# Graph attention: mask added on TensorE, plain maxima on VectorE, shorter per-engine steps; buffer rings of six and 122 edge groups instead of rings of four and 124

## The reference, cut to what matters

```python
# attention by angle, 4 layers
logits = beta * jnp.sum(h_norm[src] * h_norm[dst], axis=-1)
m = segment_max(logits, dst);  ex = exp(logits - m[dst])
out = segment_sum(ex / (segment_sum(ex, dst)[dst] + EPS) * h[src], dst)

# graph attention, 3 layers, 4 heads of 64
h = (x @ W).reshape(n, HEADS, C)
e = leaky_relu(s_src[src] + s_dst[dst], 0.2)      # s_src = <h, a_s>, s_dst = <h, a_d>
m = segment_max(e, dst);  ex = exp(e - m[dst])
out = segment_sum(h[src] * (ex / segment_sum(ex, dst)[dst]), dst) + b
```

## Time and profile before

| | us |
|---|---|
| three timed runs | 9922.85, 9924.49 (median), 9927.99 |
| profiled execution, its own time | 9927.93 |
| span, first to last instruction, of the profiled execution | 9926.2 |
| one layer of attention by angle, start to start (3896.8 to 6148.6 is three) | 750.6 |
| one layer of graph attention, start to start (6966.4 to 8902.0 is two) | 967.8 |
| PE busy over the span | 7005.6 (71%) |
| DVE busy over the span | 5926.7 (60%) |
| POOL busy over the span | 5383.8 (54%) |

### The profile page before, as it was taken

One profiled execution on the slowest core, in us unless ns is written; L12 is line 12 of the kernel. 1 busy time (PEld: TensorE's weight loads), 2 busy tenths in 40 slices (PEclk: granted clock), 3 DMA queues, 4 the chain that ended last, 5 costly groups with the idle time before them and its releaser, 6 DMA issues. The chain is left out here.

```text
span 9926.2 us, 160244 instructions
## 1 busy us (share of the span) xinstructions
PE 7005.6 (71%) x34788; PEld 5407.3 (54%) x34789; DVE 5926.7 (60%) x21625; ACT 2633.9 (27%) x6946; POOL 5383.8 (54%) x5578
## 2 busy tenths in 40 slices
PE   0003545535663982996996996996799989998997
PEld 0003445534442872885885885885466556655664
DVE  6003334442213225887887887887687768777777
ACT  0001100000000221222222222222455555555554
POOL 0675777747731112775775775774355445534553
PEclk9997557767775996998998998998677677776776
DMA  1301114453440991445445445444333323333333
GB/s 76 137 2 43 48 42 101 101 68 105 105 52 23 345 315 52 100 99 83 100 98 83 100 99 83 100 99 62 74 78 77 66 76 78 78 59 84 77 77 64
DMA packets 621385, 896.33 MB, mean 90 GB/s; under 512 B 289911, under 2 KB 427383, under 8 KB 620062
## 3 DMA queue, kind: packets, MB, share of 16 engines
q0 software_dynamic: 244928, 618.96, 28.9%
q1 hardware_dynamic: 376414, 276.94, 9.2%
HBM read 767.30 MB, written 135.40 MB: 91 GB/s over the span
## 5 line engine op out<-in xcount | busy, mean ns | idle before, releaser
L1510 POOL DMA_INDIRECT hs<-tab_agnn,rec x1984 | 1964.8, 990 | 1114.8 <-issue 593.9
L1944 POOL DMA_INDIRECT hs<-tab_gat,rec x1488 | 1406.4, 945 | 1282.6 <-DVE msg L2013 868.1
L2120 PE MATMUL psV<-msg,ohf 128*128 128x260 f32 x2976 | 1270.9, 603 | 0.8 <-DVE msg L2013 0.8
L1982 DVE CUSTOM_DVE_ANT_0 cand<-psL,neg 128x512 f32<-128x512 f32 x1488 | 991.5, 685 | 265.4 <-issue 176.4
L1531 DVE CUSTOM_DVE_ANT_0 prod<-psG,hs 128x256 f32<-128x256 f32 x1984 | 842.3, 480 | 421.1 <-DMA hs<-tab_agnn,rec 342.8
L2120 PEld LDWEIGHTS psV<-msg,ohf 128*128 128x128 f32 x2976 | 901.0, 317 | 204.1 <-issue 1.2
L1660 PE MATMUL psV<-hs,pr 128*128 128x258 f32 x3968 | 986.1, 392 | 6.2 <-DVE pr L1570 6.2
L1636 PE MATMUL psG<-HN,ohT 128*128 x3968 | 955.6, 384 | 5.1 <-ACT neg L1605 5.1
L626 PE MATMUL psT<-ident,oh 128*128 128x128 f32 x496 | 126.7, 405 | 1023.6 <-DVE oh L592 1023.6
L1636 PEld LDWEIGHTS psG<-HN,ohT 128*128 128x128 f32 x3968 | 725.6, 193 | 86.7 <-issue 6.1
L1660 PEld LDWEIGHTS psV<-hs,pr 128*128 128x128 f32 x3968 | 715.8, 190 | 89.5 <-DVE acc L1557 7.8
(11 more groups left out here) (326 smaller groups left out, 13438.2 us busy)
## 6 DMA issues: line engine op xcount, KB each, us to landing
w<-in_L_gnn_w SPq DMA_DIRECT2D x224, 512.0 KB, 6.0
fwd_d<-acc SPq DMA_DIRECT2D x10, 3224.0 KB, 44.2
fw<-fwd_d SPq DMA_DIRECT2D x124, 260.0 KB
hs<-tab_agnn,rec POOLq DMA_INDIRECT x1984
hs<-tab_gat,rec POOLq DMA_INDIRECT x1488
rec<-rec_d SPq DMA_DIRECT2D x1240, 8.0 KB, 1.7
b<-in_L_gnn_b SPq DMA_DIRECT2D x113, 128.0 KB, 6.4
x<-xbuf SPq DMA_DIRECT2D x112, 128.0 KB, 6.0
```

What stands on the lines that cost most here:

```text
L1510: nc.gpsimd.indirect_dma_start(out=hs[:, j, g, :], out_offset=None, in_=k.tab_agnn, in_offset=bass.IndirectOffsetOnAxis(ap=rec[:, j, g, 0: ...
L1944: nc.gpsimd.indirect_dma_start(out=hs[:, j, g, :], out_offset=None, in_=k.tab_gat, in_offset=bass.IndirectOffsetOnAxis(ap=rec[:, j, g, 0:1 ...
L1982: V.tensor_tensor_reduce(cand[:, m, :], psL[:, m, :], neg[:, h2, :], 1.0, -BIG, ALU.add, ALU.max, mt[:, h2, m:m + 1]).then_inc(s_lt, 1)
L2120: mm = nc.tensor.matmul(psV[:, h4, 0:W_GAT], ohf[:, h4, g, :], msg[:, h4, g, :], start=(g == 0), stop=(g == G - 1))
```

## The change

- **122 groups and rings of six.** `NG` is no longer rounded up to a multiple of the ring, `U` is 6, and `pipeline` appends the rest of the steps after the loop. The experts keep a ring of four (`UE`).
- **A row of zeros for pads.** Every gathered table gets one row more, number NP, which is zero, and pads name it. `sort_edges` sends unused records out of bounds, with a bounds check on the scatter. Logits of pads need no clamp any more: `below` goes from both attentions.
- **The mask is added on PE.** For each head a matmul of the identity with `neg` (now bf16, 512 columns, 128 rows) opens the accumulation in `psL`, and the 12-row matmul follows in it. DVE takes a plain maximum of two heads at a time.
- **No float copy of the one-hot.** PE transposes `away` in place of `oh`; ACT makes `oh` in fp32 four steps later, directly for `psV`.
- **Fewer, joined DVE operations.** Edge logits and node state share one tile `raw` and one slope operation; the block's sums are scaled in one operation and added in another; `msg` is made in one piece; ACT instead of DVE copies the peak.
- **Lags.** DVE works with lags 3, 4 and 6, PE with 1, 2, 3 and 5, ACT with 0, 1, 3 and 4.

```diff
-U = 4
+U = 6
 NG = (E + NB * (GE - 1)) // GE
-NG += -NG % U
...
+                nc.vector.memset(padrec[:, :, 0:1], NP).then_inc(s_pad, 1)
...
-                                in_=slot[:, n, g, 0:4], in_offset=None).then_inc(s_sent[n], 16)
+                                in_=slot[:, n, g, 0:4], in_offset=None, bounds_check=SPARE - 1,
+                                oob_is_err=False).then_inc(s_sent[n], 16)
...
-                                    V.tensor_tensor_reduce(cand[:, m, :], psL[:, m, :], neg[:, h2, :], 1.0, -BIG, ALU.add, ALU.max,
-                                                           mt[:, h2, m:m + 1]).then_inc(s_lt, 1)
+                                    V.tensor_reduce(mt[:, h2, m:m + 2], psL[:, m:m + 2, :], AX.X, ALU.max).then_inc(s_lt, 1)
...
+                            if add:
+                                dve.wait_ge(q.rs, flow(t6) + 1)
...
+                                V.tensor_tensor(a4, a4, b3(rs[:, j6, :], CH1), ALU.mult).then_inc(s_am, 1)
...
+                            if old:
+                                dve.wait_ge(s_leak, step_of(t + 1) + 1)
+                                V.tensor_tensor(g3(t3, h), g3(leaky, now), q3[:, :, 1, :], ALU.subtract).then_inc(q.tt, 1)
...
+                            if add:
+                                dve.wait_ge(q.v, nth(t6) + 1)
+                                dve.wait_ge(s_am, own(t6) + 1)
+                                V.tensor_tensor(acc, acc, psV[:, j6 % 2, 0:W_GAT], ALU.add).then_inc(q.u, 1)
...
-                                    nc.tensor.matmul(psL[:, m, :], sel[0:PARTS, m, :], sT[:, h1, :], start=True, stop=True).then_inc(q.b, 1)
+                                    nc.tensor.matmul(psL[:, m, :], k.identb[:, :], neg[:, h2, :], start=True, stop=False)
+                                    mm = nc.tensor.matmul(psL[:, m, :], sel[0:PARTS, m, :], sT[:, h2, :], start=False, stop=True)
```

More of the change, by code:

```diff
@@ L119, in lagged, with pipeline @@
     return i2, j2, t
-def pipeline(eng, step, drain, total=NG, numbers=None):
+def pipeline(eng, step, drain, total=NG, numbers=None, ring=U):
+    whole = total // ring
     if numbers:
         numbers.load(0)
-    for j in range(U):
+    for j in range(ring):
         step(0, j)
-    with eng.Fori(1, total // U) as i:
+    with eng.Fori(1, whole) as i:
         if numbers:
             numbers.load(i)
-        for j in range(U):
+        for j in range(ring):
             step(i, j)
-    if numbers and drain:
-        numbers.load(total // U)
-    for j in range(drain):
-        step(total // U, j)
+    for n in range(total % ring + drain):
+        if numbers and n % ring == 0:
+            numbers.load(whole + n // ring)
+        step(whole + n // ring, n % ring)
     if numbers:
@@ L1167, in experts @@
         s_ys = sem("s_ys")
-        s_out = [sem(f"s_out{n}") for n in range(U)]
+        s_out = [sem(f"s_out{n}") for n in range(UE)]
         s_gate = sem("s_gate")
@@ L1221, in step @@
                     pool.dma_start(k.ybuf_t[ds(t, 1), :, :].rearrange("a p c -> (a p) c"), y[:, n, :]).then_inc(s_out[n], 16)
-                pipeline(pool, step, 0, MT)
-                for n in range(U):
-                    pool.wait_ge(s_out[n], MT // U * 16)
+                pipeline(pool, step, 0, MT, ring=UE)
+                for n in range(UE):
+                    pool.wait_ge(s_out[n], MT // UE * 16)
             @block.vector
@@ L1265, in step @@
                         g.then_inc(s_g, 1)
-                pipeline(act, step, 1, MT)
+                pipeline(act, step, 1, MT, ring=UE)
             @block.tensor
@@ L1303, in step @@
                         mm.then_inc(s_y, 1)
-                pipeline(pe, step, 2, MT)
+                pipeline(pe, step, 2, MT, ring=UE)
 def combine(nc, k, a):
@@ new lines, in step @@
+                            top(1)
+                            if add:
+                                dve.wait_ge(q.rs, flow(t6) + 1)
+                                if not (isinstance(t6, int) and t6 < 1):
+                                    dve.wait_ge(q.u, nth(t6))
+                                a4 = acc.rearrange("p (h c) -> p h c", h=HEADS)
+                                V.tensor_tensor(a4, a4, b3(rs[:, j6, :], CH1), ALU.mult).then_inc(s_am, 1)
+                            if mid_:
+                                dve.wait_ge(s_lt, pairs(t2) + 2)
+                                V.tensor_tensor(at_block(smax, b), at_block(smax, b), mt[:, h2, :], ALU.max).then_inc(s_mx, 1)
+                                dve.wait_ge(s_mx, own(t2) * 2 + 1)
+                                V.tensor_tensor(raw[:, now, GH:], at_block(smax, b), at_block(sd, b), ALU.add).then_inc(s_mx, 1)
@@ new lines, in step @@
+                            if mid_ or old:
+                                if old:
+                                    dve.wait_ge(s_lg, own(t) + 1)
+                                if mid_:
+                                    dve.wait_ge(s_mx, own(t2) * 2 + 2)
+                                    if not (isinstance(t2, int) and t2 < 1):
+                                        dve.wait_ge(q.m, flow(t2))
+                                part = slice(0 if old else GH, GH + HEADS if mid_ else GH)
+                                V.scalar_tensor_tensor(out=leaky[:, now, part], in0=raw[:, now, part], scalar=NEG_SLOPE,
+                                                       in1=raw[:, now, part], op0=ALU.mult, op1=ALU.max).then_inc(s_leak, 1)
@@ new lines, in step @@
+                            if now:
+                                i0, _, t0 = now
+                                act.wait_ge(q.rec[j], use(i0, j) * 16 + 16)
+                                if not (isinstance(t0, int) and t0 < U):
+                                    act.wait_ge(q.t, flow(t0 - U + 1))
+                                    act.wait_ge(q.oh, nth(t0 - U + 1))
+                                for g in range(G):
+                                    ins = nc.scalar.activation(away[:, j, g, :], k.iota[:, :], ACT.Abs, bias=recf[:, j, g, 1:2], scale=-1.0)
+                                ins.then_inc(s_away, 1)
@@ L2090, in _ @@
-                        pipeline(act, step, 3)
+                                nc.scalar.activation(rs[:, j3, :], df[:, j3 % 2, :], ACT.Exp).then_inc(q.rs, 1)
+                            if last:
+                                if not (isinstance(t1, int) and t1 < 3):
+                                    act.wait_ge(q.q, flow(t1 - 2))
+                                nc.scalar.activation(flat(ohT, j1 % 3), psT[:, 0, :], ACT.Relu, bias=1.0, scale=-1.0)
+                                nc.scalar.activation(neg[:, h1, :], psT[:, 0, :], ACT.Copy, scale=-BIG).then_inc(q.ev, 1)
@@ L2092, in _ @@
+                        pipeline(act, step, 4, numbers=blocks)
                     @block.tensor
@@ new lines, in step @@
+                                pe.wait_ge(s_away, own(t1) + 1)
+                                pe.wait_ge(q.gather[j1], use(i1, j1) * (16 * G) + 16 * G)
+                                if not (isinstance(t1, int) and t1 < 1):
+                                    pe.wait_ge(q.ev, flow(t1))
+                                for g in range(G):
+                                    nc.tensor.transpose(psT[0:PARTS, 1, g * P:(g + 1) * P], hsb[:, j1, g, 2 * W_GAT:], k.identb[:, :])
+                                    mm = nc.tensor.transpose(psT[:, 0, g * P:(g + 1) * P], away[:, j1, g, :], k.identb[:, :])
```

400 lines of the change are left out of this document (170 added, 230 removed).

## The result

The changed kernel takes 10059.26 us (median of four runs, 10048.57 to 10073.25) where the kernel before takes 9923.67 on the same chip: a ratio of 1.0138, 95% interval 1.012 to 1.0155. The forecast was 9470, faster; the kernel became 136 us slower. Its profiled execution took 10055.34 us, span 10053.6.

What follows compares the result with a forecast made beforehand. PE was taken to bound graph attention and attention by angle, POOL's issue pace convolution and receiving. Terms -134 - 221 - 21 + 15 - 79 - 20 + 6 = -454 from 9927.9 gave 9474, taken as 9470 us; range 9320 to 9700.

Steps and rivals of the forecast that it cites:

- The clock: Graph attention: PE's granted clock rises from 0.72 to 0.95, 90% at the high level, giving 6.36 us of PE a group.
- The mask on PE: Graph attention: four identity matmuls add 0.96 us at the high clock, 1.81 at the low; PE's step becomes 6.08 or 10.82.
- If the matmuls of the identity don't overlap their weight loads with the 12-row ones: Named sign of being wrong, in `psL` of graph attention; eight matmuls were expected to take 1.9 us.
- DVE's own time: Graph attention: DVE busy 5.54 us a group after the change, against 5.69 before.
- PE's wait for `hs`: Graph attention: named sign that PE no longer waits for `hs`.
- DVE's wait in its chain: Graph attention: DVE waiting over 1 us in its chain would show the prediction wrong.
- The empty groups: Graph attention: twelve empty groups fall from 7.27 to the 6.7 us at which DMA alone holds them, 21 us less.
- Slower: the clock stays where it is: Rival in graph attention: 8.31 us a group, 614 us more than forecast, 10084 us in all; chance 0.07.
- break-even clock of 0.77: Graph attention: at a clock of 0.77, a step of 7.83 us, the whole gain is gone; below it the kernel is slower.
- Attention by angle: Clamp gone and ring of six ending POOL's waits: 5.25 us a group instead of 5.43, 79 us less.
- The two groups fewer: Ten passes lose two empty groups each, at 5.11 to 7.27 us a group: 134 us less.
- receiving: Receiving pass comes down from 5.29 towards 5.06 us a group: at most 25 us less, 20 taken.

Runs made afterwards that it cites:

- h3: Changed kernel with the graph attention group of the kernel before, keeping 122 groups, rings of six and the row of zeros: 9752 us, 0.9825 of the kernel before.
- h4: Old graph attention group in the new rings (h3), with 128 instead of 12 rows of weights in the matmuls into `psL`: 9708 us, 0.9778 of the kernel before.
- i1: Changed kernel with the mask back on DVE, 12-row matmuls into `psL`, exponential ahead of `sT`: 9833 us, 0.9906 of the kernel before.
- g4: Changed kernel with the mask back on DVE, 128 rows of weights for head scores, exponential ahead of `sT`: 9405 us, 0.9415 of the kernel before.
- h1: Changed kernel with 128 instead of 12 rows of weights in the head-score matmuls alone: 9388 us, 0.9455 of the kernel before.
- g2: Changed kernel with the exponential ahead of `sT` on ACT, nothing else: 10065 us, 1.0077 of the kernel before.
- g3: Changed kernel with 128 rows of weights for head scores and the exponential ahead of `sT`: 9406 us, 0.9416 of the kernel before.
- h2: Changed kernel with the identity's four `psL` matmuls ahead of the four 12-row ones, and the exponential ahead of `sT`: 9633 us, 0.9699 of the kernel before.
- series f: A slower measurement series: kernel before 11002 us; changed kernel 1.0128, with the mask back on DVE 1.0099, with 128 rows of weights 0.9959 of it.
- i2: Changed kernel with 128 rows of weights, exponential ahead of `sT`, mask of heads 2 and 3 on DVE: 9350 us, 0.9416 of the kernel before.

## Why the prediction was wrong, by its own steps

**The clock: the step that failed.** The prediction took 0.95 because "there now comes 0.96 us of the identity on 128 rows, laced with the 12-row matmuls", and took the step to be as free of gaps as that of attention by angle, which keeps 1.00. Measured is 0.83, at the high level 66% of the time. With the forecast's own steps that share gives 0.66/6.08 + 0.34/10.82, or 7.14 us instead of 6.36: 0.78 us a group of the miss. Every pair whose edit is the height alone moved: 0.72 to 0.86 (h3, h4), 0.71 to 0.97 (i1, g4), 0.83 to 0.98 (changed, h1), 0.82 to 0.97 (g2, g3). The earlier trace rows already held a sign of it: the 12-row matmuls at the high clock were followed by a low stretch. I read that as a gap that the identity would fill. Of what the prediction said doesn't hold the clock up, the runs bear out the 12-row matmuls; the 8-column ones are in h1 too, at 0.98.

One thing stays open. Whoever makes the weights taller also hides the loads at the edges of `psL`, and those inside it where the mask is on PE: `psQ` starts 0.30 to 0.32 us behind the last matmul of `psL` where that has 12 rows (h3, h2, changed), and 0.216 behind one of 128 (h1, g3). Height and these short waits were never changed one without the other. The number of exposed loads in a step doesn't order the clocks, though: two go with 0.71 (i1) and with 0.87 (h2), eight with 0.83 (changed).

**The mask on PE: mis-sized.** The term of 0.96 us at the high level came out as 2.54 - 0.96 = 1.58 us, since 0.10 us of weight load is exposed at each change of height. "If the matmuls of the identity don't overlap their weight loads with the 12-row ones" was named as what would prove me wrong, and it is what happened. The step is 6.55 at the high level. At the low one its parts are 3.74 for `psV`, 1.7 for the transposes, 8 x 0.535 for `psL` (a spacing that the three layers have 84 times among some 2,300, and the window not once) and 1.75 for `psQ`, about 11.5. 0.66/6.55 + 0.34/11.5 gives 7.67: 0.53 us more. PE is idle for 16.1 us in the window, 0.18 us a group (9.6 us of it in seven waits marked "issue", the heads of turns), 7.85 together against 7.82 measured. So by this estimate the miss of 1.4 us a group is 0.78 clock, 0.53 loads, and the rest idle time, mostly heads of turns. The two are not independent: taking out six of eight exposed loads (h2) brought 1.0 us and 0.04 of clock. That both come from the 12 rows is shown by h1, which changes their number alone and takes 671 us less than the changed kernel.

**The other forecasts of graph attention.** DVE's own time was right and a little high (5.19 for 5.54), its maximum exact (1.22), PE's wait for `hs` did go. DVE's wait in its chain, over 1 us, was named as a sign of being wrong and came (1.6 us a group), but g2 shows that it cost nothing. The empty groups did not fall to 6.7 us at full DMA: their gathers come 7.7 to 8.4 us apart in the three layers, with PE busy 92.55 of 95 us and the DMA engines 0.60 (7765 to 7860 us). DMA didn't hold them before either: the earlier trace rows has it 0.57 busy there, and 0.99 only in attention by angle, from which the 6.7 was taken. The rival "Slower: the clock stays where it is" was right in sign and half right in mechanism: the break-even clock of 0.77 was worked out for steps without exposed loads, and with them 0.83 is not enough; its 8.31 us a group is nearer to the 7.82 than the forecast is. I gave it 0.07.

**Transposes and loads.** The prediction weighed for that rival what the Trainium skill, TensorE: Matmul & The Clock Gate, section Part 4: PE-mode transpose, says of transposes. No run has transposes alone, but h1 does the same ones, 1.16 us of each 5.70, and has a clock of 0.98, so they did not pull it down there. On the loads, the Trainium skill, on the same page, section The mechanism, says that a weight load overlaps with a running matmul only where the two use different groups of rows; the section also names a background buffer for weights as a second way. The measurement decides: loads of equal height are hidden (0.216 us spacing, 128 rows behind 128 rows), loads of different height are not (0.32).

**Attention by angle.** -92 for -132. The mean spacing of `psV` over groups 10 to 100 is 5.42 us, 5.44 before: POOL's waits fell and the pace did not, because PE does 5.08 us a step and pays 0.8 and 2.7 us in turn at the heads of turns, now and then 4.3. I had taken 5.25 and left these heads out. The 23 us a layer come from the end instead: two empty groups, and only the last four or five of twelve empty groups run at 6 to 7 us, where eleven did before. That the six slots of lead are the reason is likely and not shown.

**Ends, receive, bounds check.** The two groups fewer came out in the convolution (11.5 us for 13) and by half in send (5 for 10); receiving gave 13 of 34. The check cost some 5.5 us in the scatters (972 ns each for 958; 6 us forecast). 7 us more between experts and attention are not explained. h3 is the sum of all this: 175 us.

## What to carry to other kernels

- A matmul with few rows of weights can cost PE more than its columns: in four pairs with the same columns the granted clock was 0.71 to 0.83 with 12 rows and 0.86 to 0.98 with 128. Padding the weights with zero rows is free in columns; where the tile is zeroed once, it was worth 7% of this kernel (1.0138 to 0.9455).
- Don't interleave weights of different height: each change exposed a load of 0.10 us. Group them, or make them equal.
- Ask of a wait whether the bound engine stands behind it. 1.6 us a group of DVE's waiting was worth nothing while PE was full, and a higher clock for the old group gained 45 us and not 200, because PE then waited for DVE's chain.
- Don't judge an edit where something else holds the pace: in series f the mask on PE seemed to cost nothing, and between g2 and i1 it cost 73 us a layer.

The change of rows alone beats both kernels: h1 takes 9388 us where the kernel before takes 9927, ratio 0.9455. The fastest is i2, with the exponential ahead of `sT` and half the mask on DVE: 9350 us where the kernel before takes 9933, ratio 0.9416.

## What the runs showed of the hardware that was not expected

- The spacing of bf16 matmuls of 512 columns at the high clock is 0.216 us with 12-row weights in a row and with 128-row weights in a row, and 0.310 to 0.323 where 12 and 128 alternate; 0.535 at the low clock, against 0.427 with equal height.
- The granted clock was higher with taller weights at equal columns in every pair, and it rose while PE became less busy (0.72 at 95% to 0.86 at 82%).
- The same kernel before took 9927 and 11002 us in two series with the same chip number, 9933 and 11033 in two others. Graph attention of the changed kernel, where PE is full, was nearly untouched (1066.5 us a layer against 1047.9). The edit that gave 0.9455 of the kernel before in one series gave 0.9959 and 0.9908 in the slower ones.
